# Moving the context halves and projections to other slots in a decoder layer's attention kernel

## The reference

```python
# self attention: log_pen[b, q, k] is worked out from a gate, the same for all heads
scores = einsum('bhqd,bhkd->bhqk', q, k) / sqrt(16) + log_pen[:, None]
ctx = einsum('bhqk,bhkd->bhqd', softmax(scores), v)
x = layernorm(x + ctx)
# cross attention: keys and values from ctx_1024, an additive mask
logits = einsum('bhqd,bhkd->bhqk', q, k) / sqrt(16) + mask * -1e9
x = layernorm(x + einsum('bhqk,bhkd->bhqd', softmax(logits), v) @ Wo + bo)
# feed-forward: 256 -> 704 -> 256, inputs, weights and hidden values rounded to 8 bits
x = layernorm(x + ffn(x))
```

## Time and profile before

| | us |
|---|---|
| median of three runs | 885.67 |
| lowest, highest of them | 885.41, 898.06 |
| the profiled execution's own time | 889.29 |
| its span, first to last instruction | 887.2 |
| PE busy | 715.0 (81%) |
| DVE busy | 653.7 (74%) |
| ACT busy | 484.2 (55%) |
| POOL busy | 290.5 (33%) |

### The profile page before, as it was taken

The page is one execution under the profiler, slowest core; times in us unless marked ns, Lnnn a source line. Parts: engine busy times, 40 slices in busy tenths (PEclk is TensorE's granted clock), DMA queues, the critical chain, the costliest instruction groups (busy, mean ns, idle before and its releaser), DMA issues.

```text
span 887.2 us, 12849 instructions
## 1 busy us (share of the span) xinstructions
PE 715.0 (81%) x4372; PEld 281.7 (32%) x4374; DVE 653.7 (74%) x1704; ACT 484.2 (55%) x800; POOL 290.5 (33%) x257
## 2 busy tenths in 40 slices
PE   6087888998788989999798899997788799975753
PEld 3052223343222243444232333442222234332231
DVE  3988775675689776778995666689787587727996
ACT  3213455545435767744456677445456576863634
POOL 6103545535436213334453032446223000001414
PEclk9588899999889989999899999999899899996966
DMA  3532123220311304212223123133111420000002
GB/s 101 152 103 91 47 67 91 57 62 1 98 42 51 107 24 120 81 27 50 59 57 92 38 75 91 38 83 108 57 38 37 106 62 19 6 1 1 0 1 95
DMA packets 34896, 54.00 MB, mean 61 GB/s; under 512 B 4368, under 2 KB 25872, under 8 KB 34832
## 3 DMA queue, kind: packets, MB, share of 16 engines
q1 hardware_dynamic: 32912, 51.61, 20.4%
q10 hardware_dynamic: 1920, 1.57, 1.1%
HBM read 36.91 MB, written 14.68 MB: 58 GB/s over the span
## 4 chain that ended last, share of the span: by engine, by line
PE 44%; DVE 32%; ACT 8%; issue 7%; POOL 7%; DMA 2%; SPq 1%; ACTq 0%; POOLq 0%; DVEq 0%
DVE unused L929 9%; PE ps L1454 9%; PE ps L1409 9%; PE ps L1429 6%; PE ps L1396 5%; PE ps L1312 5%; POOL probs L653 4%; PE ps L1389 3%; ACT probs L821 2%; PE ps L1433 2%; PE ps L1434 2%; POOL rest L663 2%; DMA KS<-parts_kc 2%; DVE x L966 1%; DVE pen_a L986 1%
## 5 line engine op out<-in xcount | busy, mean ns | idle before, releaser
L1409 PE MATMUL ps<-KS,QS 96*128 96x512 bf16 x512 | 204.6, 401 | 91.8 <-DVE mx L929 68.3
L821 ACT ACTIVATE probs<-ps 128x512 f32<-128x512 f32 x256 | 149.3, 596 | 168.9 <-PE ps L1434 109.2
L653 POOL TENSOR_TENSOR probs<-probs,penT 128x512 f32<-128x512 f32 x128 | 165.5, 1312 | 207.9 <-ACT probs L821 207.8
L929 DVE CUSTOM_DVE_ANT_0 unused<-ps,lp 128x512 bf16<-128x512 f32 x256 | 171.1, 686 | 69.7 <-PE ps L1409 65.6
L1429 PE MATMUL ps<-QS,KS 108*128 108x512 bf16 x512 | 200.0, 393 | 6.9 <-ACT probs L821 6.8
L821 ACT ACTIVATE probs<-ps,mask_col 128x512 f32<-128x512 f32 x256 | 166.4, 688 | 55.9 <-PE ps L1429 54.4
L929 DVE CUSTOM_DVE_ANT_0 unused<-ps,mask_rest 128x512 bf16<-128x512 f32 x192 | 129.0, 685 | 43.1 <-PE ps L1409 41.5
L1409 PEld LDWEIGHTS ps<-KS,QS 96*128 96x128 bf16 x512 | 50.6, 99 | 243.1 <-DVE mx L929 150.6
L663 POOL TENSOR_TENSOR rest<-proj,parts 128x512 f32<-128x512 f32 x32 | 38.8, 1212 | 161.3 <-ACT parts L734 160.7
L1454 PE MATMUL ps<-probs,v_s 128*32 128x256 f32 x1024 | 84.5, 402 | 6.0 <-POOL probs L653 5.3
L1454 PE MATMUL ps<-probs,v_c 128*32 128x256 f32 x1024 | 82.7, 396 | 0.6 <-ACT probs L821 0.6
(11 more groups left out here) (185 smaller groups left out, 964.4 us busy)
## 6 DMA issues: line engine op xcount, KB each, us to landing
parts_qs<-parts SPq DMA_DIRECT2D x8, 384.0 KB, 2.7
parts_ks<-parts SPq DMA_DIRECT2D x8, 384.0 KB, 2.5
QS<-parts_qs SPq DMA_DIRECT2D x16, 192.0 KB
KS<-parts_ks SPq DMA_DIRECT2D x16, 192.0 KB
parts_kc<-parts SPq DMA_DIRECT2D x8, 384.0 KB, 2.6
parts_qc<-parts SPq DMA_DIRECT2D x8, 384.0 KB, 2.9
QS<-parts_qc SPq DMA_DIRECT2D x16, 192.0 KB
KS<-parts_kc SPq DMA_DIRECT2D x16, 192.0 KB
```

Of the source, the lines that this page charges most:

```text
L653: g.tensor_tensor(probs[:, T % NP, :], probs[:, T % NP, :], penT[:, MUL_KT.index(kt), :], ALU.mult)\
L821: s_.activation(probs[:, T % NP, :], ps[:, EXP_BANKS[T % 3], :], ACT.Exp, bias=bias)\
L929: v.tensor_tensor_reduce(out=unused[:, i % 2, :], in0=ps[:, MAX_BANKS[i % 2], :], in1=lp[:, t, :] if kind == "s" else mask_row(b), scale=1 ...
L1409: mm(ps[:, MAX_BANKS[i % 2], :], QS[0:SK, slot, j, t * P:(t + 1) * P], KS[0:SK, slot, j, :], start=True, stop=True).then_inc(max_scores, 1)
```

## The change

The two context halves of a key tile go from slots 2 and 3 of four to slots 1 and 3. The last two halves of a group go from slots 1 and 2 of the next step to 1 and 3, ACT's copy from 2 to 3, the turn (`norm`) from 4 to 5, where the job `m` stands already. The slots for second halves of projections go from 1, 5, 9, 13 to 2, 6, 10, 14, and in these slots the first half is issued two slots ahead, where that slot has no bank job. The other bank jobs may go to even slots.

```diff
--- before.py
+++ after.py
@@ -101,8 +101,9 @@
 
 
 
-QUIET_SLOTS = (0, 1, 4, 5, 8, 9, 12, 13)
-LONG_SLOTS = (1, 5, 9, 13)
+QUIET_SLOTS = (0, 2, 4, 6, 8, 10, 12, 14)
+LONG_SLOTS = (2, 6, 10, 14)
+CONTEXT_SLOTS = (1, 3)
 
 
 def long_job(job):
@@ -129,8 +130,8 @@
             at = [(0, ("shift", s.shift, 0)), (0, ("shift", s.shift, 1)), (1, ("shift", s.shift, 2)),
                   (1, ("shift", s.shift, 3)), (5, ("m", s.shift)), (6, ("load_m", s.shift))] + list(at)
         if s.norm is not None:
-            at = [(1, ("last_context", s.norm, 0)), (2, ("last_context", s.norm, 1)), (2, ("oT", s.norm)),
-                  (4, ("norm", s.norm))] + list(at)
+            at = [(1, ("last_context", s.norm, 0)), (3, ("last_context", s.norm, 1)), (3, ("oT", s.norm)),
+                  (5, ("norm", s.norm))] + list(at)
         for slot, job in at:
             s.items[slot].append(job)
         for lo, hi, task in tasks:
@@ -148,7 +149,10 @@
         for slot in range(1, TG):
             if any(job[0] in BANK_JOBS for job in s.items[slot - 1]):
                 continue
-            s.items[slot - 1] += [("half", *job) for job in s.items[slot] if long_job(job)]
+            first = slot - 1
+            if slot > 1 and slot in LONG_SLOTS and not any(job[0] in BANK_JOBS for job in s.items[slot - 2]):
+                first = slot - 2
+            s.items[first] += [("half", *job) for job in s.items[slot] if long_job(job)]
         steps.append(s)
 
     add(("s", 0, 0), stacks=[2, 3], fetch=[("xT", 1)],
@@ -1471,8 +1475,8 @@
                         max_tile(s.p1 + (i + 2) // TG, (i + 2) % TG)
                     if s.p2 is not None:
                         exp_tile(s.p2, i)
-                        if i % GH >= 2 and i > GH:
-                            context(s.p2, i // GH - 1, i % GH - 2)
+                        if i % GH in CONTEXT_SLOTS and i > GH:
+                            context(s.p2, i // GH - 1, CONTEXT_SLOTS.index(i % GH))
                     for job in s.items[i]:
                         do(job)
```

## The result

The changed kernel takes **906.91 us** (median of 4 runs, 902.73 to 910.32) against 888.25 us for the kernel before on the same chip: a ratio of **1.0175, 95% interval 1.0127 to 1.0223**. Run again later with six runs it took 906.2 us, ratio 1.0192 (1.014 to 1.0244). It is slower, by about the 2% that counts as a change here, and the forecast of 877.5 us was wrong by 29 us and in its sign; the time lies outside the range of 866 to 893. The profiled execution took 905.67 us, its span is 903.4 us against 887.2.

A forecast was written before the change was run, and what follows sets the result against it. PE was taken to bound quiet steps, DVE most of the penalty steps. Gains of 11.7 us less losses of 3.5 gave 881.1 from the profiled 889.3; runs' median lay 3.6 lower, so 877.5 us, range 866 to 893.

The forecast's parts named there:

- Quiet steps: Cross-attention steps without penalties: even spacing removes a PE wait of 0.30 us, 14 times, 4.2 us gained.
- Projections parted: At some 13 places a projection's half no longer stands beside a context half, 0.1 us each, 1.3 us gained.
- chain: Three steps: projection's remainder comes after POOL's fourth product, the exponential ahead of `middle`; 4.5 us gained, from 0 to 7.
- One wait for a DMA: Before the first maxima of ("c", 3, 0): one context half less ahead of `q c 3`'s second part, 0.7 us gained.
- steps with penalties: Some five steps where DVE is the bound: context halves spread over PE's waits, 1 us gained in all, up to 5.
- The earlier context half: Self attention, key tiles 0 and 2: slot 14's tiles come behind the wait for POOL; 1.5 us lost, between 0 and 7.8.
- Of the other six most are covered: Six halves near POOL's end, outside the untied chains: most delays hidden by other waits; 5.2 us if uncovered.
- The rival's waits (8 to 20 us): PE's waits for POOL before context halves, forecast to grow from 5.3 us to between 8 and 20.
- The end of a group: Later copy `oT` meets the next group's earlier first half: 0 to 0.53 us in each of ten steps, 1 us lost.
- Clock: Stretches at 1.2 GHz after PE's idle spells: 1 us lost, between 8 lost and 5 gained.
- POOL becomes the wait of self attention: Some 12 self-attention quads lose 0.87 us each, plus lower clock: 8 us slower, 894; chance 0.17.
- the conditions I gave for failure: Forecast fails if PE's waits for POOL grow beyond 20 us or the granted clock moves by more than 0.01.

The follow-up runs named there:

- cross_inner: Kernel before, with context halves in slots 1 and 3 inside cross-attention groups alone; 893.88 us, ratio 1.0063.
- chain_even: Kernel before, three projections one slot later, context halves in slots 1 and 3 except those that wait for POOL; 886.56 us, ratio 0.9965.
- before_chain: Kernel before, with only three projections (k s 1 0, k c 0 0, q c 0 0) one slot later; 885.8 us, ratio 0.9973.
- after_end_before: Changed kernel with the end of a group as before (last halves in slots 1 and 2, copy 2, turn 4); 886.66 us, ratio 0.996.
- before_mul_early: Kernel before, with only the halves of POOL's key tiles in self attention moved to slots 1 and 3; 897.74 us, ratio 1.0091.
- mul_late: Changed kernel with the halves that wait for POOL's products back in slots 2 and 3; 893.32 us, ratio 1.0041.
- after_norm6: Changed kernel with the turn of oT in slot 6, whereby projection k was halved again and m came ahead; 889.14 us, ratio 0.9973.
- after_turn_first: Changed kernel with the turn of oT issued ahead of the context half in slot 5 instead of behind it; 901.52 us, ratio 1.0115.

## Why the prediction was wrong

- *Quiet steps, 4.2 gained.* The mechanism held to a hundredth (3.40 to 3.10 for four slots). That the sum would reach the end didn't: cross_inner is 0.6% slower and chain_even no faster than before_chain; in both, two steps with bank jobs beside the moved halves lose 1.1 us each, more than three quiet ones gain. In the changed kernel the new end of a group takes 0.35 back in the quiet step with p2 = ("c", 2, 3): 14.9 us in after_end_before, 15.2 here.
- *Projections parted, 1.3; chain, 4.5.* The chain was right in mechanism: `middle` waits its 2.01 us behind the fourth product. The three steps fell by 7.8 us in the profile, and by 5.4 with the chain alone, which is worth 0.27% (2.4 us) of the whole time, not clear of noise. "Where slot 0 takes the whole projection (before slot 5's) nothing is saved and nothing lost on PE" holds for slots 0 and 1 (3.37 us before, 3.26 after) and left out the second projection, which `LONG_SLOTS` moves from slot 5 to a whole one in slot 6: the four steps are 1.2 to 1.5 us longer each, 5.2 together, which was put at nothing.
- *One wait for a DMA, 0.7; steps with penalties, 1.* The wait went from 5.40 to 5.56 us, so nothing came of the first. No run separates the second.
- *The earlier context half, 1.5 lost.* "Of the other six most are covered" is the first step that failed. The rival's waits (8 to 20 us) were right: 17.9 us in 11 waits, 12.6 more than before, which is beyond the bound of 7.8. I covered them with DVE's being late, from one timeline, and in that very step the 0.8 us came in full. What the earlier halves cost depends on the kernel around them: nothing measurable with the turn in slot 4 and the chain untied (0.9968 to 0.996), 0.9% with the turn in slot 4 and the chain tied (before_mul_early), 1.5% with the turn in slot 5 (1.0041 to 1.0192), where I had charged 1.5 us, 0.2%.
- *The end of a group, 1 lost.* The second and larger failure, the sentence "`norm` and `m` now stand in one slot, with a half: slot 5 grows, and DVE's division with it, but DVE has two maxima in hand". DVE had one: the row maximum of slot 5's tile, then the division. Its waits grew by 22.8 us. ACT's copy, for which the 1 us was charged, cost nothing more (5.8 us of waits before, 5.7 after). Putting the old end back is worth 2.3% (0.996 against 1.0192); I had charged 0.1%.
- *Clock, 1 lost.* Up to 8.6, just beyond the 8 named as its bound. In one stretch of three steps it was all of the loss of the first profile, and the second had 3 us less there.
- *The rival "POOL becomes the wait of self attention"*, 894 at a chance of 0.17, had the sign and one of the mechanisms. It fell short because it priced POOL by itself and kept the other terms, the end of a group at 1 us among them. Its tests were nearly met (waits of 17.9 us against 20, clock 0.008 against 0.010), so the conditions I gave for failure didn't ring although the forecast had failed.

**What stays open.** The two losing terms cost more together than apart: 0.996 to 0.9968 with neither or only POOL's halves early, 1.0041 with the new end alone, 1.0192 with both. The granted clocks of the four profiles go the same way (0.921, 0.915, 0.913, 0.905), so part of it is the clock's. Not all: at 0.907 mul_late took 896.2 us and the changed kernel 904.7 and 906.1, and after_norm6 took 886.6 to 890.9 at 0.906 to 0.907. Yet step by step the loss is hard to place: from after_end_before to the changed kernel the 13 steps with the full clock in both profiles grow by 4.1 us together, the other 18 by 12.4. Whether the rest is the turn behind a half that waits for POOL isn't shown; after_turn_first, which takes that away, moved the time by 0.8% with an uncertainty as large.

## What to carry to other kernels

When work moves in an in-order schedule, write out for each instruction moved what now stands behind it on its own engine, and what the planner then does with the jobs that this slot used to hold; here the two together were worth more than the bubbles that the change removed. A term priced "covered" needs its cover shown at each place where it occurs, and a gain of 0.3 us in each quiet step has to be set against the steps in which the moved work meets other jobs. An experiment that moves one job can let the planner move a second one, so read the plan of each variant before its time is given a cause. Read an instruction's shortest and longest duration beside its mean: a cost of up to 53.8 us of DVE's time stood there, and PE's waits bore DVE's name for what POOL had done.

## What the runs showed of the hardware

**POOL blocks DVE.** Rows of the kernel before by tile (shortest, median and longest ns), then of the one with short products:

```profile
L915 DVE SCALAR_TENSOR_TENSOR mrest<-mx,mparts x32: 174/175/1196, 61.3 to 763.1; 128x16 f32<-128x16 f32 x32
...
L919 DVE TENSOR_TENSOR mparts<-mrest,mparts x32: 174/176/2207, 62.4 to 763.5; 128x16 bf16<-128x16 f32 x32
```

```profile
L915 DVE SCALAR_TENSOR_TENSOR mrest<-mx,mparts x32: 174/175/231, 62.1 to 708.9; 128x16 f32<-128x16 f32 x32
...
L919 DVE TENSOR_TENSOR mparts<-mrest,mparts x32: 174/176/2207, 63.1 to 709.3; 128x16 bf16<-128x16 f32 x32
```

L919 works on 16 columns. Before, it took 174 to 177 ns in the 19 cases in which no POOL instruction ran. In 11 cases it started some 0.1 us behind the start of a product with the penalties, took 1187 to 1200 ns and ended 0.03 us after that product. In one it started 0.07 us ahead of the product and took 174 ns. The longest, 2207 ns, stood under another POOL instruction (L677, 2.36 us), and is there with short products too; under these the others took 291 ns at most. L970 above took 1.35 us under a product and 0.40 right after it. The row maxima, which read a score tile in PSUM and one operand in SBUF, took 686 ns in either kernel. The Trainium skill, "SBUF — State Buffer", section "Who interferes with whom", says that a DVE instruction with two SBUF inputs contends with a GpSimd instruction that reads SBUF, and that one in a 2-port mode shares a port pair with GpSimd which whoever issues first holds for the whole instruction. By that rule L919 is blocked, a `tensor_scalar` as L970 can be, and the maxima aren't; the trace agrees. The prediction had read the penalty steps as bound by DVE's own work; up to 53.8 us of DVE's 653.7 was this.

**The clock differs between executions of the same program.** The step with p1 = ("s", 0, 1), in two profiles of the changed kernel:

```profile
59.60:81.80 22.20, 16.26 (x47) 7.55 (x45) 16.90 (x52) 6.93 (x12) 4.83 (x4) 0.73 0.09 29
```

```profile
59.90:79.70 19.80, 13.74 (x47) 5.71 (x46) 17.10 (x53) 6.49 (x11) 4.84 (x4) 0.83 0.11 36
```

The same 47 instructions took PE 16.26 and 13.74 us. One profile against one other doesn't settle a cause worth 2 us. Over whole executions it is more: in 29 of the kernel before on one chip the mean granted clock lay between 0.902 and 0.919 and the time between 885.4 and 898.1 us, nine at 0.918 with 885.4 to 889.0, the two at 0.902 and 0.904 with 897.3 and 897.4. What sets the clock of an execution isn't shown.
